# Causal mask moved into unused rows of the attention products, with the placed queries carried by transfers

## The reference

```python
def _L0_xattn_ref(q, k, v, W, b, mask):           # q: layernorm(x) [32,256,256]; k, v: ctx [32,77,256]
    H = 16; dh = 16
    scores = einsum('bhqd,bhkd->bhqk', qh, kh) / sqrt(dh)
    causal = triu(ones((Sq, Sk)), k=1)            # key position later than query position: masked
    scores = where(merged == 1, -inf, scores)     # merged: causal or padding
    attn = softmax(scores, axis=-1)
    out = einsum('bhqk,bhkd->bhqd', attn, vh)
    return out.reshape(B, Sq, D) @ W.T + b
x = x + tanh(g_xattn) * _L0_xattn_ref(_layernorm(x), ctx, ctx, W, b, mask)
x = x + tanh(g_ffn) * _L0_ffn_ref(_layernorm(x), ...)   # shared FFN + top-2 of 8 experts
```

## Time and profile before

| | us |
|---|---|
| median of 3 runs (1114.1 to 1115.92) | 1115.81 |
| the profiled execution's own time | 1116.76 |
| its span, first to last instruction | 1115.0 |
| PE busy | 1066.6 (96%) |
| DVE busy | 835.2 (75%) |
| POOL busy | 520.2 (47%) |
| ACT busy | 472.6 (42%) |

### The profile page before, as it was taken

How to read it: one execution, slowest core, us unless ns; L and a number is a source line. 1 busy time by engine, 2 the same in 40 slices (tenths; PEclk the granted TensorE clock), 3 DMA queues, 4 the chain that set the end, 5 groups by cost and what they waited for, 6 DMA issues and landing times.

```text
span 1115.0 us, 22178 instructions
## 1 busy us (share of the span) xinstructions
PE 1066.6 (96%) x7283; PEld 897.8 (81%) x7283; DVE 835.2 (75%) x1859; ACT 472.6 (42%) x722; POOL 520.2 (47%) x617
## 2 busy tenths in 40 slices
PE   5779999999999999999999999999998999999997
PEld 3557888788788888888887778888887888888886
DVE  6677886987987888878868765466443788888886
ACT  4566656555565666566565432233221111111110
POOL 6434447456465465474483333000002566666564
PEclk9899999999999999999999999999999999999999
DMA  7888856666765767576465113787553555554451
GB/s 144 179 173 129 201 136 120 149 131 146 122 152 126 119 142 141 122 143 156 111 96 135 31 38 127 241 261 225 183 171 116 161 164 153 164 158 155 151 169 64
DMA packets 108130, 161.84 MB, mean 145 GB/s; under 512 B 29101, under 2 KB 72943, under 8 KB 108017
## 3 DMA queue, kind: packets, MB, share of 16 engines
q1 hardware_dynamic: 96244, 122.40, 47.2%
q0 software_dynamic: 11776, 38.03, 11.3%
HBM read 76.43 MB, written 52.12 MB: 115 GB/s over the span
## 4 chain that ended last, share of the span: by engine, by line
PE 84%; DVE 9%; issue 3%; ACT 2%; POOL 1%; DMA 0%; POOLq 0%; ACTq 0%; DVEq 0%
PE ps L781 16%; PE ps L726 13%; PE ps L828 13%; PE ps L743 7%; PE ps L830 6%; PE ps L648 4%; PE ps L636 4%; PE ps L679 3%; PE ps L813 3%; PE ps L601 3%; PE ps L657 2%; DVE mneg L1230 2%; PE ps L631 2%; PE ps L607 1%; PE ps L702 1%
## 5 line engine op out<-in xcount | busy, mean ns | idle before, releaser
L828 PE MATMUL ps<-regr,gh 128*128 x600 | 221.5, 407 | 0.1
L905 ACT ACTIVATE Pt<-ps,pbias 77x1024 f32<-77x1024 f32 x128 | 141.5, 1106 | 89.8 <-PE ps L636 86.3
L830 PE MATMUL ps<-regr,gl 128*128 x600 | 169.9, 283 | 0.0
L828 PEld LDWEIGHTS ps<-regr,gh 128*128 128x128 f32 x600 | 113.8, 190 | 23.8 <-issue 0.5
L995 ACT ACTIVATE gh<-ps 128x512 fp32r<-128x512 f32 x75 | 44.8, 599 | 204.8 <-PE ps L813 204.8
L1420 POOL TENSOR_TENSOR gl<-gf,gh 128x512 fp32r<-128x512 f32 x64 | 82.5, 1291 | 99.2 <-ACT gh L867 98.9
L1230 DVE TENSOR_REDUCE mneg<-ps 128x8 f32<-128x616 f32 x128 | 100.3, 792 | 22.6 <-PE ps L601 15.8
L830 PEld LDWEIGHTS ps<-regr,gl 128*128 128x128 f32 x600 | 114.0, 190 | 0.0
L726 PE MATMUL ps<-x2h,winh 128*128 128x512 f32 x256 | 108.1, 422 | 0.6 <-DVE OHR L1110 0.6
L726 PE MATMUL ps<-x2h,winl 128*128 128x512 f32 x256 | 101.0, 394 | 0.0
L726 PE MATMUL ps<-x2l,winh 128*128 128x512 f32 x256 | 100.8, 394 | 0.0
(11 more groups left out here) (208 smaller groups left out, 2655.2 us busy)
## 6 DMA issues: line engine op xcount, KB each, us to landing
regr<-regr SPq DMA_DIRECT2D x96, 256.0 KB, 5.9
y_dram<-Pt SPq DMA_DIRECT2D x64, 256.0 KB, 2.1
regf<-in_x SPq DMA_DIRECT2D x32, 256.0 KB, 2.9
x<-in_x SPq DMA_DIRECT2D x32, 256.0 KB, 4.3
y_dram<-res SPq DMA_DIRECT2D x32, 256.0 KB, 2.4
regr<-regr SPq DMA_DIRECT2D x96, 77.0 KB, 6.8
x_dram<-x2h SPq DMA_DIRECT2D x14, 512.0 KB, 3.0
x_dram<-x2l SPq DMA_DIRECT2D x14, 512.0 KB, 3.8
```

The costliest lines, as they stand in the source:

```text
L828: e.matmul(o, gh2[:, k % 3, fc, :], w2v[:, bass.ds(val, 1), fc, :, :].rearrange("p o h d -> p (o h) d"), start=fc == 0, stop=False, skip_g ...
L830: m = e.matmul(o[:, 0, :], gl2[:, k % 3, fc, :], w2v[:, bass.ds(val, 1), fc, 0, :].rearrange("p o d -> p (o d)"), start=False, stop=fc == ...
L905: e.activation(Pt[0:K, 4 * k:4 * k + 4, :].rearrange("k (n j) t -> k n (j t)", n=2), bank_of["sc", b, k][0:K, :, :], ACT.Exp, bias=pbias[: ...
```

## The change

- `KR` is 128 instead of 100: the `scores` product contracts over 128 rows. Rows 100 to 127 of `Kst` hold -2^127 where a key is later than token `r` (`r` = 0 to 27), and rows 100 to 127 of `Xs` hold a one at token `r`, so the mask of the first 28 tokens (`TOK`) comes out of the product. The mask matmuls (L631) cover tokens 28 to 76 only: 98 moving columns instead of 154.
- `xM` takes the place of `xTh` as weights in `max`. For head group `q` its 64 rows of queries are placed beside 64 rows that are an identity for tokens 0 to 63; the matching 64 rows of `Kbd` hold `caus`. The mask matmuls (L607) cover the last 12 keys only (`LATE` = 64): 48 moving columns instead of 308.
- `xM` is one buffer. For batch 0 ACT writes it with two copies; for every other batch SP issues two transfers of 128 KB from `xTh` (stage `xM`, slot 6, right after `xT` and ahead of `queries`), and `max` waits for both (`xm`).
- `xTh` and `xTl` have one buffer instead of two, so ACT's copy `xT` of batch `b` waits until the three `queries` transfers of batch `b-1` have landed.
- POOL's `keys` pieces are 64 rows by 616 (four heads, both channel halves) instead of 128 rows by 616; both stand in slot 3, the second waits for the first and for scatters already issued, and PE waits for both.
- At the start: DVE clears `xM` and writes its identity rows, ACT copies `caus` into `Kbd` (two copies of 64 rows by 1232), POOL clears rows 96 to 127 of both halves of `Xs` and ACT copies a piece of `ident` there; the clearing of `Vau` moves to a later stage; the constant `own` is 32 by 154 instead of 4 by 2464. Two semaphores of POOL's roots are merged.

```diff
-KR = 100
+KR = 128
+TOK = 28
+LATE = 64
@@ phase_one
-        put(i, ((2, "norm", 0), (6, "xT", 0), (10, "queries", 0)))
+        put(i, ((2, "norm", 0), (6, "xT", 0), (6, "xM", 0), (10, "queries", 0)))
-                4: ((7, "keys", 0), (7, "keys", 1))}.get(i, ((1, "keys", 0), (3, "keys", 1))))
+                4: ((7, "keys", 0), (7, "keys", 1))}.get(i, ((3, "keys", 0), (3, "keys", 1))))
@@ buffers
-        xTh = carve(P, [2, 2, S])
-        xTl = carve(P, [2, 2, S])
+        xTh = carve(P, [2, S])
+        xTl = carve(P, [2, S])
+        xM = carve(P, [2, 2, S])
@@ SP
+                if stage_ == "xM" and b:
+                    e.wait_ge(s["xTh"], b + 1)
+                    e.wait_ge(s["mm"], 4 * b)
+                    for j in range(2):
+                        e.dma_start(xM[64 * j:64 * j + 64, j, :, :].bitcast(F), xTh[64 * j:64 * j + 64, :, :].bitcast(F)).then_inc(s["xm"], 16)
@@ PE
                 elif stage_ == "max":
                     if k == 0:
-                        e.wait_ge(s["xTh"], b + 1)
+                        if b == 0:
+                            e.wait_ge(s["xTh"], 1)
+                            e.wait_ge(s["ks1"], 2)
+                        else:
+                            e.wait_ge(s["xm"], 32 * b)
+                        e.wait_ge(s["kbd"], 2 * b + 2)
                     for q in range(2):
-                        m = e.matmul(o[:, q], xTh[:, h, c, t * P:(t + 1) * P], Kbd[:, g, c, 4 * q:4 * q + 4, :], start=True, stop=t == 1)
+                        m = e.matmul(o[:, q], xM[:, q, c, t * P:(t + 1) * P], Kbd[:, g, c, 4 * q:4 * q + 4, :], start=True, stop=t == 1,
+                                     skip_group_check=True)
...
-                            m = e.matmul(o[:, q], identb[:, :], caus[:, :].unsqueeze(1).broadcast_to([P, 4, K]), start=False, stop=True)
+                            m = e.matmul(o[:, q, :, LATE + 1:K], identb[:, :],
+                                         caus[:, LATE + 1:K].unsqueeze(1).broadcast_to([P, 4, K - LATE - 1]), start=False, stop=True,
+                                         skip_group_check=True)
...
                     for n in range(2):
-                        e.matmul(pair[0:K, n, :].rearrange("k (j t) -> k j t", j=2)[:, :, 0:K], identb[0:K, 0:K],
-                                 cauT[:, :].unsqueeze(1).broadcast_to([K, 2, K]), start=True, stop=False, skip_group_check=True)
+                        e.matmul(pair[0:K, n, :].rearrange("k (j t) -> k j t", j=2)[:, :, TOK:K], identb[0:K, 0:K],
+                                 cauT[:, TOK:K].unsqueeze(1).broadcast_to([K, 2, K - TOK]), start=True, stop=False, skip_group_check=True)
@@ ACT
                 elif stage_ == "xT":
                     e.wait_ge(s["xT"], b + 1)
-                    if b >= 2:
-                        e.wait_ge(s[f"xs{h}"], 48 * (b // 2))
-                        e.wait_ge(s["mm"], 4 * (b - 1))
+                    if b == 0:
+                        e.wait_ge(s["dcon"], DCON["rows"])
+                        for j in range(2):
+                            e.activation(xM[64 * j:64 * j + 64, j, :, :], v[64 * j:64 * j + 64], ACT.Copy)
+                    else:
+                        e.wait_ge(s[f"xs{1 - h}"], 48 * ((b + 1) // 2))
+                        if b >= 2:
+                            e.wait_ge(s["xm"], 32 * (b - 1))
+                    e.activation(xTh[:, :, :], v, ACT.Copy).then_inc(s["xTh"], 1)
@@ POOL
+                    else:
+                        e.wait_ge(s["kbd"], 2 * b + 1)
+                        if scattered[0]:
+                            e.wait_ge(s["scat"], 16 * scattered[0])
+                    rows, m = slice(64 * k, 64 * k + 64), slice(4 * k, 4 * k + 4)
+                    e.tensor_tensor(Kbd[rows, b % G, :, m, :],
+                                    khi[rows, b % G * 2:b % G * 2 + 2, :].bitcast(F).unsqueeze(2).broadcast_to([64, 2, 4, K]),
+                                    own8[rows, m].unsqueeze(1).unsqueeze(3).broadcast_to([64, 2, 4, K]), ALU.mult).then_inc(s["kbd"], 1)
```

More of the change, by code:

```diff
@@ L1223, in vector @@
                     e.wait_ge(s["xTh"], b + 1)
[L1224 removed]
+                    low(xTl[:, :, :], ("xT", b, 0), xTh[:, :, :]).then_inc(s["xTl"], 1)
                 elif stage_ == "max":
@@ L1581 @@
         _np.diff([p_[0] for p_ in pairs]), _np.diff([p_[1] for p_ in pairs])]).astype(_np.float32)
-    own = _np.zeros((4, 2, H, K), _np.float32)
+    own = _np.zeros((32, 2, K), _np.float32)
     for r_ in range(4):
         own[r_, r_ % 2] = 1.0
-    arrays["own"] = own.reshape(4, -1)
+    for r_ in range(TOK):
+        own[4 + r_, :, r_ + 1:] = NEGS
+    arrays["own"] = own
     nc = _bacc.Bacc("TRN2", target_bir_lowering=False, num_devices=1)
```

70 lines of the change are left out of this document (45 added, 25 removed), and 4 rows, old and new, of the table names.

## The result

| | us | ratio to before |
|---|---|---|
| before, median of 6 runs (1114.1 to 1116.84) | 1115.74 | |
| after, median of 6 runs (1154.03 to 1159.71) | 1155.94 | 1.0368 [1.0355, 1.0381] |
| forecast | 1128.5, range 1112 to 1137 | |

The change makes the kernel 40 us slower. The direction was forecast, the size was not: the measured time is 27 us above the forecast. The profiled execution of the changed kernel has a span of 1154.0 us.

The account below looks back on a forecast made before the run. PE was taken to set the pace in the dense part, and a chain of waits with SP's queue full in the start. 1116.8 + 20 (start) - 7.2 (dense) = 1129.6, as a median 1128.5; range 1112 to 1137.

Parts of the forecast that it names:

- the two extra waits: POOL's keys pieces waiting for its own first piece and for scatters: hidden by idle time, nothing or 1 us.
- The start: Batches 0 to 5: late xM transfers delay the first products, a loss of 20 us, between 10 and 27.
- Batch 1: xM waits for batch 0's queries, then a full queue; product at about 30 instead of 18.3, loss 9 us.
- Batch 3: xM waits for batch 2's queries and stands behind FFN weights; product at 59.6 instead of 50.7, loss 8 us.
- The dense gain: Shorter mask matmuls on PE save 4.9 + 0.7 for max and 1.6 for scores, 7.2 us in all.
- the split by pieces: Max masks from batch 5: piece 1 gains 4.9 us, piece 0, mostly waiting for DVE's bank, 0.7.
- The upper bound of 14: Dense part, PE: most the shorter masks could gain, 12 for max and 6.1 for scores less the start's share.
- the bound that I took from L657: PE pace set by weight loads, some 0.9 ns a weight column, so 0.07 us for 77 columns.
- B: Rival: in the start, transfers go past the queue and lose 11.5, dense gains 14; 1113.3 us, chance 0.16.
- C: Rival: they cancel; dense columns count in full, 14 gained, and the start costs 15; 1117 us, chance 0.10.
- D: Rival: dense part loses too, xM late by 1 us in 13 odd batches; 1141 us, chance 0.12.
- the margin of 1.1 us: Odd batches of the dense part: time left between xM's landing and its first product, hidden but narrowly.

Follow-up runs that it names:

- e15: The kernel before, unchanged, run again on a faster chip as base for the runs beside it; 1114.88 us.
- e18: Changed kernel with DVE writing the late second keys pieces and ACT copying xM for batches 0 to 4; 1125.27 us, ratio 1.0081.
- e16: The changed kernel as it is, on a faster chip beside e15; 1155.41 us, ratio 1.0363.
- e17: Changed kernel, but DVE writes the second keys piece in batches with fresh scatters, on the chip of e16; 1136.69 us, ratio 1.0190.
- e1: Changed kernel, but DVE writes the second keys piece in batches with fresh scatters, on a slower chip; 1142.91 us, ratio 1.0180.
- e2: Kernel before with both keys pieces in slot 3 and the second waiting for scatters already issued; 1133.56 us, ratio 1.0086.
- e6: Changed kernel with even batches' keys pieces moved ahead of the scatters from batch 6 on, order alone; 1144.99 us, ratio 1.0192.
- e4: Changed kernel with two buffers again for xTh and xTl, xM still by transfer; 1155.72 us, ratio 1.0283.
- e7: e6 with PE's mask matmuls at full width again; 1154.86 us, ratio 1.0264.
- e12: e4 with the xM transfers of batches 1 to 4 issued from ACT's queue instead of SP's; 1145.64 us, ratio 1.0212.
- e5: The changed kernel as it is, on a slower chip; 1150.96 us, ratio 1.0251.
- e9: Changed kernel with DVE writing the late second keys pieces and ACT copying xM for batches 0 to 4, slower chip; 1134.56 us, ratio 1.0092.
- e10: e9 with ACT instead of DVE writing the late second keys pieces; 1143.45 us, ratio 1.0192.
- e11: Changed kernel with no xM transfer: ACT writes xM for all batches into two buffers, and the late keys too; 1150.31 us, ratio 1.0241.

## Why the prediction was wrong

**The failed step: "the two extra waits ... are covered by its idle time: nothing, or 1 us".** On the chip of e15 to e18 it measured 18.7 us (e16 less e17 by medians; 20.8 in the dense stretch of the traces). Two things in it were wrong. I priced a scatter's landing by nothing at all, though the second piece waits for it; it takes 7.5 us in a stretch where the DMA engines are full. And I set POOL's mean idle share (48 of 100 us in the earlier trace rows) against the wait, though in one iteration of four POOL has eight scatters of 1 us within 16 us, and the keys, the bias, a low part and the root of the second norm between them: for 19 us it has no pause over 0.3 us. The forecast did name what is behind ("a low part that PE wants"), but not the root, and gave it no row. e1 and e17 take the piece with its wait off POOL, e2 puts the wait alone, with the first piece's later slot, into the kernel before: the same chain of waits comes and goes with it, and e6, where the scatters that it waits for have landed by then, has no such chain either. The most direct test, POOL's own piece in its place without the wait for scatters, was not run; e1 and e17 also take a piece of work off POOL.

**The start was forecast at 20 and measured 20.4 to 21.1.** Its parts, from the first products of batches 0 to 5 in the first comparison: 2.4, 10.2, 0.6, 4.4, 1.9 and 0.9, where the forecast had 0, 9, 0.5, 8, 2 and 0, and 0.5 for the clock. Batch 1 is right with its mechanism, at 30.93 for "about 30". Batch 3's product came at 68.27, 17.6 later than before for "some 18", but less of that was its own, 4.4 for 8: the `queries` of batch 2 landed at 59.7 us, 8.6 later than in the earlier trace rows though batch 1 had lost 12.6, and `xM` landed 7.3 us after its issue, not 11.9. The first product's 2.4 was forecast as mostly absorbed; PE waits there for POOL's second piece of keys. The sum held because such errors cancel, which is luck. The parts are not firm either: between e15 and e16, the same two kernels on another chip, they are 2.7, 11.7, -2.9, 7.2, 2.0 and 0.5.

**What of the start is the transfer.** The copies in place of transfers give back 10.2 us of 22.1 (e18 against e17 in the traces; 11.4 by medians). The other 12 stay without any transfer of batches 1 to 4. With the copies batch 1's first product runs at 21.48, but its fourth pair of products at 27.68, in the timeline of e18:

```profile
27.68 0.88 PE L638 MATMUL ps<-regr 128*128 128x308 f32 x2 [3.76 <-DVE mneg L1300]
```

Its chain that ended last leads there through the copy of `xTh`, which waits for the landing of batch 0's `queries`, and through DVE's low part behind it:

```profile
16.82 7.08 DMA regr<-regr
23.92 0.61 ACT regr L946
...
26.91 0.73 DVE mneg L1300
...
27.68 0.88 PE ps L638 x2
```

That is the single buffer's price, which the forecast counted only as part of `xM`'s delay. This is read from the chain and not tested: two buffers alone gave nothing (e4), and two buffers together with the copies were not run. They would be the next thing to try.

**The dense gain was forecast at 7.2.** From the first mask product of a pair to the second, e16 is shorter than e15 by 5.6 us for `max` and 2.3 for `scores`, 7.9 in all; from the second of `max` to the next matmul the wait for the bank takes 0.8 back. In piece 1, which has no such wait, the second holds 0.026 us where it held 0.132, so the split by pieces was right. A gain of 2.7 to 3.4 stays in the dense stretch of e17 and e18. There DVE has six more pieces of keys to write, and behind a pair of piece 0 the next matmul starts 0.51 to 0.53 us later where it was 0.31 in e15. By e7 against e6 the masks' width is worth 9.9 us of the whole. So 7.2 was about right as the pace of PE, and less of it arrives. The upper bound of 14 does not come out of its own terms: 12 for `max` and 27 of 32 batches of the 6.1 for `scores` are 17. The pair ahead of L646 was forecast to hold 0.05 to 0.10 and holds 0.06. Two L646 start 0.051 us apart on average and 0.048 in the median, the 42 ns of their 98 columns and little more; the bound that I took from L657, 0.07 for 77 weight columns, is too high for these. The Trainium skill ("TensorE: Matmul & The Clock Gate", section "LDWEIGHTS (loading the stationary operand)") has a load take its columns over 1.2 GHz, by which I estimate 64 ns for 77 columns. The trace does not agree with it here; the measurement decides.

**The rivals.** B (transfers pass the queue) decided from a landing before 25 us; it came at 30.9. e12 shows that even in a queue of its own it comes at 28.4. C needed the start at 15. D forecast a late `xM` in odd batches; in the traces of the changed kernel no product from 100 to 640 us waits for a DMA, so the margin of 1.1 us held. D had a loss in the dense part of about the right size from the wrong cause, and none of the rivals had POOL.

**What stays open.** The scatter stall costs about 19 us on the chip of e15 to e18 and about 8 on the slower ones (e5 less e1), and the changed kernel 40 and 27. No trace of the kernel before exists on a slower chip, but three kernels were traced on both kinds, and the sums of distances tell where the chips differ. The changed kernel's dense stretch is 2.9 us shorter on the slower chip (e5 against e16). Without the wait it is longer there: by 4.7 us in e1 against e17, and by 10.4 in e9 against e18. So it seems that the slower chips lose time of their own in the dense stretch, and that the wait for scatters hides it; each of these is one traced execution. In e9 10.2 of the 10.4 us lie ahead of the products of `max` (L638) and the transposes of the maxima (L654); what makes these late there no run tells. The 2 us of e16 to e18 in the rest, behind 640, are no effect: the first comparison's trace of the kernel before has 1.9 of them against that of e15.

## What to carry to other kernels

A wait added on an engine that issues its work in a fixed order is not paid from that engine's mean idle time. Price it where it falls: when was what it waits for issued, how long does such a landing take in the DMA load of that very stretch, and which later instruction of the same engine does another engine need next. Where the delayed instruction itself does no harm, the next one behind it that another engine needs can.

Before moving work to an engine with a low busy share, look whether a full engine waits for it piece by piece (e10, e11): a share of 42% was no room.

## What was not expected of the hardware

A scatter on GpSimd's queue took 7.5 us from issue to the end of the wait for it while the DMA engines were full. The 256 KB of the queries, on a queue of their own, still took 7 us in such a stretch. And two chips (e5, e16) gave ratios of 1.025 and 1.036 for the same two kernels, further apart than either interval is wide.
